# Scores two pairs ahead: issued behind the first transpose group of a pair where they stood behind the second

## What is computed

```python
q = _w8a8_linear(x, wq, bq).reshape(B, N, H, D).transpose(0, 2, 1, 3)
k = (cond @ wk.T + bk).reshape(B, L, H, D).transpose(0, 2, 1, 3)
v = (cond @ wv.T + bv).reshape(B, L, H, D).transpose(0, 2, 1, 3)
scores = jnp.einsum('bhnd,bhld->bhnl', q, k) * inv_sqrt_d + mask[:, None]
attn = jax.nn.softmax(scores, axis=-1)
o = jnp.einsum('bhnl,bhld->bhnd', attn, v)
```

## Time and profile before

| | us |
|---|---|
| median of 3 runs | 983.55 (983.32 to 983.77) |
| the profiled execution | 986.56 |
| its span, first to last instruction | 984.8 |
| TensorE matmuls busy | 914.5 (93% of the span) |
| VectorE busy | 556.1 (56%) |
| ScalarE busy | 564.8 (57%) |

### The profile page before, as it was taken

The page is one execution under the profiler, slowest core; times in us unless marked ns, Lnnn a source line. Parts: engine busy times, 40 slices in busy tenths (PEclk is TensorE's granted clock), DMA queues, the critical chain, the costliest instruction groups (busy, mean ns, idle before and its releaser), DMA issues. The chain is left out here.

```text
span 984.8 us, 19351 instructions
## 1 busy us (share of the span) xinstructions
PE 914.5 (93%) x7803; PEld 783.0 (80%) x7803; DVE 556.1 (56%) x1054; ACT 564.8 (57%) x976; POOL 74.5 (8%) x83
## 2 busy tenths in 40 slices
PE   5945989999999999999999999999999999989995
PEld 3534579898989898989898988888888888877773
DVE  2695465656564656565655565656565556553424
ACT  2513166767575657565766666666666665653442
POOL 0021000000000000000000000000000000063453
PEclk9965699999999999999999999999999999989998
DMA  6009557575757565666666666666766676400001
GB/s 177 7 23 267 150 132 171 128 172 133 161 135 159 145 150 146 147 155 141 159 150 158 139 160 151 158 139 159 154 159 138 159 152 140 93 15 1 2 1 37
DMA packets 67816, 126.13 MB, mean 128 GB/s; under 512 B 23568, under 2 KB 52408, under 8 KB 67512
## 3 DMA queue, kind: packets, MB, share of 16 engines
q1 hardware_dynamic: 66384, 124.66, 53.1%
q10 hardware_dynamic: 1344, 0.23, 0.2%
HBM read 46.30 MB, written 4.65 MB: 52 GB/s over the span
## 5 line engine op out<-in xcount | busy, mean ns | idle before, releaser
L1248 ACT ACTIVATE probsT<-ps_T 125x448 f32<-125x448 f32 x384 | 195.2, 544 | 181.8 <-PE ps_T L1122 181.8
L1349 DVE CUSTOM_DVE_ANT_0 scores<-ps_scores,mask_sb 112x1500 f32<-112x1500 f32 x128 | 219.7, 1716 | 79.5 <-PE ps_scores L1111 75.1
L1122 PEld LDWEIGHTS ps_T<-ident,scores 112*125 112x125 f32 x1536 | 200.6, 189 | 17.6 <-ACT probsT L1248 3.1
L1122 PE MATMUL ps_T<-ident,scores 112*125 112x112 f32 x1536 | 207.9, 271 | 2.1 <-ACT probsT L1248 2.0
L1238 ACT ACTIVATE scores<-scores,shift 112x1500 f32<-112x1500 f32 x128 | 197.1, 1540 | 0.9 <-DVE shift L1349 0.9
L1091 PE MATMUL ps_proj<-room,wkvT 128*128 128x500 f32 x576 | 158.5, 411 | 6.2 <-DVE room L1332 3.3
L1136 PE MATMUL ps_out<-probsT,v_sb 125*32 125x112 f32 x3072 | 161.3, 262 | 0.0
L1099 PE MATMUL ps_proj<-wkvT,room 128*125 128x256 f32 x1152 | 159.7, 289 | 0.5 <-DVE v_sb L1327 0.4
L1136 PEld LDWEIGHTS ps_out<-probsT,v_sb 125*32 125x32 f32 x3072 | 145.8, 111 | 15.6 <-issue 10.6
L1099 PEld LDWEIGHTS ps_proj<-wkvT,room 128*125 128x125 f32 x1152 | 146.5, 189 | 10.3 <-issue 4.3
L1336 DVE SCALAR_TENSOR_TENSOR room<-ps_proj,xbk,room 128x500 fp32r<-128x500 f32 x96 | 70.7, 737 | 125.0 <-ACT room L1233 124.9
(11 more groups left out here) (252 smaller groups left out, 616.8 us busy)
## 6 DMA issues: line engine op xcount, KB each, us to landing
k_stack<-room SPq DMA_DIRECT2D x384, 187.5 KB, 4.0
ctx_rows<-in_ctx SPq DMA_DIRECT2D x48, 500.0 KB
mask_sb<-in_mask_BxSxS_ff SPq DMA_DIRECT2D x32, 328.1 KB
q_stack<-q_hi SPq DMA_DIRECT2D x32, 112.0 KB, 5.3
q_hi<-k_stack SPq DMA_DIRECT2D x4, 448.0 KB, 3.8
q_lo<-k_stack SPq DMA_DIRECT2D x4, 448.0 KB, 4.0
q_stack<-q_lo SPq DMA_DIRECT2D x16, 112.0 KB, 5.3
ctx_rows<-in_L_ffn_mask_idx SPq DMA_DIRECT2D x1, 1024.0 KB, 5.7
```

The lines of the kernel that those rows point to most:

```text
L1122: last = nc.tensor.transpose(ps_T[0:LT, (TB * t + k) % 2, j * PN:(j + 1) * PN], scores[:, t % 2, (k * TC + j) * LT:(k * TC + j + 1) * LT], ...
L1248: nc.scalar.activation(probsT[:, t % 2, k * TC:(k + 1) * TC], ps_T[0:LT, (TB * t + k) % 2, 0:TC * PN].rearrange("p (j n) -> p j n", j=TC), ...
L1349: nc.vector.tensor_tensor_reduce(out=split(scores[:, t % 2], NC), in0=ps_scores[0:PN, :, 0:LC], in1=split(mask_sb[:, a], NC), scale=-1.0, ...
```

## The change

In `batch` of the TensorE block the call of `scores_of` goes up by one place: it stood behind the groups 0 and 1 of the pair's transposes, and stands behind group 0.

```diff
                             transposes(b, t, 0)
-                            transposes(b, t, 1)
                             if t + 2 < NP:
                                 scores_of(b, half, a, t + 2, True)
                             elif project:
                                 scores_of(b + 1, half + a, 1 - a, t + 2 - NP, True)
+                            transposes(b, t, 1)
                             transposes(b, t, 2)
```

## The result

The changed kernel takes 1007.96 us in the median (1006.38 to 1008.22), the kernel before 983.43 in the same comparison: a ratio of 1.0247, 95% interval 1.023 to 1.0265. The forecast was 1012.1, in a range of 1006 to 1020.

A forecast was written before the change was run, and what follows sets the result against it. TensorE was taken as the bound, busy 709.94 of 719.00 us in the steady attention part. Costs of 27.0 + 1.5 = 28.5 us on 986.56 gave 1015.1 profiled, so a median of 1012.1, range 1006 to 1020.

The forecast's parts named there:

- T1: Second of a pair's three transpose groups in TensorE's order, four transposes; the scores move ahead of it in 126 pairs.
- What the scan waits for: First duo's even pair: VectorE's scan at 419.69 is released by the last transposes, ended 419.65, not the scores, ended 419.22.
- T2: Third and last of a pair's three transpose groups on TensorE.
- Rival 1: Attention stage, faster: scores release the scan, so it starts 0.94 us earlier in first duos; 6.5 us gained, 977.1; chance 0.03.
- The price of T1: TensorE in each pair: eight transposes take 1.02 us, so one group was priced at 0.51.
- the four duos: Odd pairs of a batch's duos: costs of 0.51, 0.42, 0.36 and 0.51 us, 1.80 a batch, 27.0 in 15 batches.
- The range: Whole kernel: least 1005.9, idle time swallowing 6.1 us; most 1020.1, 62 odd pairs each paying 0.59 us.
- The last batch: Odd pairs there: first duo 0, second 1.02 at half clock, third 0.51, fourth without scores; sum 1.53 us.
- Does the lateness stay: Behind a pair's last transposes, copy, values, exponential and later units all follow them, so the whole cost is passed on.
- Rival 2: Attention stage, no change: TensorE gives the cost back at later waits that don't follow the last transposes; 983.6; chance 0.02.
- rival 3: Attention stage, slower by more: a gap lowers TensorE's clock in every batch, 41.6 us more, 1053.7; chance 0.05.
- The count of waits: TensorE's listed waits for the scan before the scores: about 60 times instead of 18, about 20 us instead of 6.8.

The follow-up runs named there:

- early in even pairs only: Against the kernel before, the scores go ahead of the second transpose group in even pairs only: 984.26 us, ratio 1.0001.
- second trace of before: The kernel before run and profiled once more with nothing changed: 982.45 us, span 980.7.

## Why the prediction was right, and where its sizes were off

**The direction and the mechanism** held: no cost in even pairs, the cost in odd pairs, by a wait for the scan that T1 used to fill. The experiments with the scan shortened show it, and that it follows each duo's own distance to the scan.

**What the scan waits for** was read rightly from line 1343 and the 0.04 us behind T2, against the releaser that one row of the waits names. Another row of the same view, of the kernel before, names the transposes, for the memset that carries the scan's waits; 15 of its 18 cases are the fourth duos:

```profile
DVE wait_cell L1348 <- PE ps_T L1122: 23.9, 18, 1.5
```

Rival 1 is out: the scan of the first duo's even pair did not come forward, and 427.22 stands 0.05 behind T2 again. With a third buffer it does come forward, by 0.26 us in a first duo, and even then the new order is no faster than the old one (steady parts of 715.48 and 714.98 us). The 71.4 us in the earlier trace rows are of a part of the span; over the whole span that row has 75.1.

**The price of T1** was the term that was mis-sized. I took half of the 1.02 us that eight transposes show. But the drawn end of a row has a tail of its own: four transposes show 0.59 and eight 1.02, so a group more is 0.43. In the same way scores stand 0.36 behind T0, not 0.28. With 0.43 the four duos are 0.43, 0.34, 0.28 and 0.43, together 1.48, and 15 batches 22.2. Measured: 0.43, 0.33, 0.28 and 0.43, and 21.97 in all. The distances to the scan, 0.15 of them unavoidable, were right in each duo.

**The range** held, but not by the reasoning of its lower bound. That bound let idle time elsewhere swallow 6.1 us of the cost, and next to nothing was (21.97 us in the steady part where the corrected sum gives 22.2); the cost was smaller because T1 and the last batch had been priced too high. The upper bound counts 62 odd pairs, and there are 63 of the 126.

**The last batch** was given 1.53 and took 0.8. Its first duo's cost was absorbed as said: T2 of the next pair, which waited 1.03 us for ScalarE's copy, waited 0.61. In the second duo, priced at 1.02, the scores still ran at full clock, and T1 and T2 together took 1.61 us, where one group at half clock had been drawn with 1.02. From the transposes of that odd pair to those of the next duo's even pair it is 10.29 us before (863.69 to 873.98) and 10.46 after (884.54 to 895.00), 0.17 more. From there to the end of the batch it is 15.73 and 16.36, 0.63 more where 0.51 was priced. The two places in the changed kernel:

```profile
882.80 0.69 PE L1122 MATMUL ps_T<-ident,scores 112*125 112x112 f32 x4 [0.61 <-ACT probsT L1248]
...
887.62 0.91 PE L1111 MATMUL ps_scores<-k_stack,q_stack 96*112 96x500 f32 x3 [2.49 <-DVE shift L1349]
...
888.36 1.61 PE L1122 MATMUL ps_T<-ident,scores 112*125 112x112 f32 x8
```

A stretch of half clock here is not a fixed part of the kernel: of the 13 traces, the second one of before and that of "early in even pairs only" have none. So the 0.8 holds for these two executions only.

**Does the lateness stay:** it does. With one duo changed, only that duo is longer, and the steady part is longer by 15 times that: 6.54 for 15 x 0.43, 4.10 for 15 x 0.28. Rival 2 is out.

**The clock** stayed at 1.00 in the steady part, with a gap of 0.64 us in each first duo, so rival 3 did not come. For this stretch the trace does not bear out what the Trainium skill says of transposes (TensorE: Matmul & The Clock Gate, Part 4: PE-mode transpose), that they do not count as busy for the clock in the way matmuls do. Score matmuls stand in the stretch too, so what transposes alone would do, no run here shows. A lower clock was seen outside the steady part: 0.91 in the last batch, and in the changed kernel 0.86 just ahead of the steady part:

```profile
116.71:130.61 13.90, 12.08 (x60) 0.86 0.56 121
```


**The count of waits** was wrong in form: 33 times, not about 60. In second and third duos the scores come only 0.12 and 0.05 us behind T0's drawn end (441.82 and 455.50), and the view lists no wait there. The view counts a wait 0.23 us shorter than the scores are held (0.64 for the 0.87 from 428.22 to 429.09), where 0.31 had been taken. Its 17.9 us are near the 20 forecast, but they grew by 11.1 where the kernel lost 22: the drawn busy time grew too, from 710.07 to 719.21, with the same matmuls, since T0's tail is now drawn into the wait instead of under the next group. This holds for the duos whose scores had not waited before: the kernel changed in third duos alone shows 713.43 us busy, the one changed in first duos alone 710.09.

**The base.** The sum was 28.5; with the right terms it is 22.2 + 0.8 = 23.0, and the medians differ by 24.5. The profiled execution of before stood 3.0 us above its median, that of after 0.3, and the second trace of before shows 3.0 us that come and go in the last batch, most of them with the clock. That the remaining 1.5 us are of this kind is argued, not shown.

## What to carry to other kernels

In an in-order queue, work ahead of an instruction that waits covers the wait. Before such an instruction is moved up, look at how far behind its release it stands now: it can move by that distance less the handover (0.15 us here) and no more, and what it is moved past beyond that is added to the path. If the engine that it feeds also waits for something that stays behind the moved instruction, as the scan waits for T2 here, moving up gains nothing even where it is free. To price a few instructions out of a merged row, take the difference of two rows of different count, not a share of one.

## What the hardware showed that I had not expected

The drawn length of a group of matmuls has a constant part: 0.59 us for four transposes and 1.02 for eight, so 0.16 beside 0.43 for each group. The scores follow 0.36 us behind the start of a group that is drawn with 0.59, so the idle time that the trace shows at such a wait is too short by 0.23 us.

In the even pairs of second and third duos, and of nearly all first duos, the scan starts 0.04 to 0.05 us behind the drawn end of T2; in fourth duos it is 0.17 in all 15 batches, here in the changed kernel (T2, memset, scan), and why is open. Behind the score matmuls it is 0.21, when those release it.

```profile
413.63 1.02 PE L1122 MATMUL ps_T<-ident,scores 112*125 112x112 f32 x8
...
414.77 0.06 DVE L1348 MEMSET wait_cell<- 112x1 f32 x1 [1.35 <-PE ps_T L1122]
414.82 1.72 DVE L1349 CUSTOM_DVE_ANT_0 scores<-ps_scores,mask_sb 112x1500 f32<-112x1500 f32 x1
```

The same code runs its last batch at either level of TensorE's clock. With 2.38 us of idle time before the scores of the second duo the granted clock fell to 0.50; in the second trace of before the idle time there is 2.03 us and the clock stays at 1.00:

```profile
865.73 0.91 PE L1111 MATMUL ps_scores<-k_stack,q_stack 96*112 96x500 f32 x3 [2.03 <-DVE shift L1349]
...
867.31 2.49 PE L1136 MATMUL ps_out<-probsT,v_sb 125*32 125x112 f32 x48
```

The values there take 2.49 us where they took 4.18. The length of this idle time does not decide it alone: in the kernel with early scores in first duos it is 2.11 us and the half clock comes, in the one with early scores in even pairs it is 2.13 and it does not.

```profile
872.48 1.56 PE L1111 MATMUL ps_scores<-k_stack,q_stack 96*112 96x500 f32 x3 [2.11 <-DVE shift L1353]
```

```profile
866.48 0.91 PE L1111 MATMUL ps_scores<-k_stack,q_stack 96*112 96x500 f32 x3 [2.13 <-DVE shift L1353]
```
